# Two graph layers: counts in three slots in the first pass, one-hots in the fourth slot's room, selection matrices with edges side by side

## The chip, the cores and the metric

One core of a Trainium2 chip runs the whole kernel. The metric is device microseconds of one execution. Before the change it is 4469.84 us, the median of three runs (4464.91 to 4476.29).

## What is computed

Two graph layers over 12500 nodes of 64 features and 212500 edges, sorted by destination. Cut to what matters:

```python
h = maximum(layernorm(x), 0)
msg = h[src] + edge_attr                        # first layer, 64 features per edge
agg = segment_sum(msg, dst)
h = relu(agg @ W1 + b1) @ W2 + b2               # 64 -> 128 -> 64
x = x + batchnorm(h) * gamma + beta
h = maximum(layernorm(x), 0)
for W, b in ((W11, b11), (W12, b12)):           # second layer, two convolutions
    h = relu(segment_sum((h @ W)[src] * dis[src] * dis[dst], dst) + b)   # self loop added
x = x + graphnorm(h)
```

`dis` is one over the root of a node's degree. So three times the rows of a node table are summed over the edges that end in a node: passes 0, 1 and 2.

## The kernel before

**How a pass sums.** The nodes are cut into 100 tiles of 125. A table row is held as three bf16 parts (high, middle, low), 192 columns, and a column of ones counts edges. A pass has two ways to sum. A *dense window* (125 destination nodes) multiplies a matrix of edge counts, 125 x 12500 in fp8, with the whole table that lies in SBUF: 100 products (L1102, "app"). The other edges go in *groups* of 1280 (128 partitions x 10): GpSimd gathers their rows by ten indirect DMAs (L1265), VectorE makes a selection matrix of 96 columns per ten edges of a partition (L964, "S"), and ten products (L1124) add them. `DENSE = (54, 69, 69)` windows are dense in passes 0, 1 and 2. In pass 0 all 167 groups need a selection matrix, since the edge features of every edge are summed too: SP loads 320 KB of them (L1299, "edges"), VectorE makes the middle and low parts (L980, "rest1", "rest2") and ten products (L1117) sum them. 79 of the 167 groups of pass 0 are gathered as well, alternating with groups that are not, and the last ones are not.

**How the counts are built.** All windows of pass 0 and 17 windows of pass 1 are built on the chip, the others are loaded from the `counts` memory (1600 KB each, L1288). A window takes 32 products (L1084, "bld") of two one-hot matrices, both by VectorE: `oh` of 200 columns (L954, one per product, `NOH = 6` buffers) and `ob` (L951, one for four products, `NOB = 3` buffers). Two products fill one of two PSUM banks (`NBANK = 2`), and ScalarE copies the pair into the window's slot (L1204, "evict"). There are `NA = 4` slots of counts, `part(o_A, slot, n_A)`. A finished window is stored for the passes behind it (L1303, "keep").

**What follows the sums.** VectorE folds the three parts of a window (L996, L997) or group (L987), TensorE turns the fold (L1189, L1185), and VectorE adds it to `acc` (L1020, L1015). In pass 0 each finished run of 500 nodes goes through the perceptron: L1137 and L1140 on TensorE, then relu (L1213), hout (L1217), hmean (L1222) and hvar (L1227) on ScalarE.

**What sets the order.** `make_plan` writes every engine's list by hand: each piece of work has a due time in plan units (one window is `NAP = 25` units, the products of one window 1 unit per four), and an engine's list is sorted by it. In pass 0 a one-hot is due 3.3 units ahead of its product, S 7.0, the edge DMA 12.5, rest1 5.2 and rest2 4.2 ahead of the group's products. Within its list an engine waits on semaphores: a one-hot for the product that used its buffer (`p_bld`), a product for its one-hot (`v_oh`) and for the eviction two pairs back (`a_ev`), the edge DMA for the products of group v-2 (`p_q`), a slot for the products of the window that had it (`p_app`) and for its store (`st_cnt`). After pass 0, SP loads x again into `H`, which is the room of slots 2 and 3 (L1338); VectorE uses it from L1602 on, behind the batch norm.

## Time and profile before

| | |
|---|---|
| median of three runs | 4469.84 us |
| the profiled execution | 4486.21 us, its span 4484.9 us |
| pass 0 (first fold at 219, last at 1880) | about 1670 us from 210 us |
| batch norm, second layer norm, until the first fold of pass 1 | 148 us |
| pass 1, pass 2 | about 1232 us, 1140 us |
| PE busy | 3012.4 us, 67% of the span |
| DVE busy | 1926.5 us, 43% |
| POOL busy | 1861.6 us, 42% |
| ACT busy | 796.3 us, 18% |
| mean granted TensorE clock | 0.81 |

The profile is one execution. Its groups ("lines") give busy time, the mean duration of one instruction, and the idle time of the engine just before the group's instructions with what ended it. PE is TensorE's matmul, PEld its weight load, which runs beside the matmul before it. Busy times of PE groups overlap each other, since a matmul's record holds its latency. "remote" and "issue" are waits whose end the profile can't put down to a recorded instruction. The granted clock is 1.00 at 2.4 GHz and 0.50 at 1.2 GHz.

### The profile page before, as it was taken

The numbers are of one execution on the slowest core, as the hardware profiler recorded it, in microseconds if no ns is written. First come the engines' busy times: TensorE is split into PE (matmuls) and PEld (weight loads), VectorE is DVE, ScalarE is ACT, GpSimd is POOL, SyncE is SP. The second block draws the span as 40 slices with busy tenths as digits, with TensorE's granted clock in tenths as the row PEclk, the third lists the DMA queues.
The fourth block names the chain that finished last, engine by engine and source line by source line (L and its number), as shares of the span: only waits on it lengthen the run. The fifth ranks groups of instructions, "written<-read, shape, count | busy, mean of one in ns | idle before, by whom it ended". The sixth has DMA issues, their size and how long they took to land.

```text
span 4484.9 us, 66591 instructions
## 1 busy us (share of the span) xinstructions
PE 3012.4 (67%) x26545; PEld 2766.3 (62%) x26545; DVE 1926.5 (43%) x4856; ACT 796.3 (18%) x1708; POOL 1861.6 (42%) x1895
## 2 busy tenths in 40 slices
PE   1366676676666667737777777777847777776777
PEld 1365565566556556636666676666846666666667
DVE  9476676767667667742333332323301111111112
ACT  6122222222222223332111111111100000000000
POOL 4554444545444442032444433444134444444441
PEclk9988788878877788858778878888968778878878
DMA  5243333434334333443333333333443333333334
GB/s 125 78 115 100 96 111 99 118 96 116 99 94 114 96 111 101 118 124 119 113 99 114 127 99 127 100 116 126 140 120 113 126 111 127 113 111 119 119 126 123
DMA packets 359879, 504.29 MB, mean 112 GB/s; under 512 B 302486, under 2 KB 302679, under 8 KB 334736
## 3 DMA queue, kind: packets, MB, share of 16 engines
q1 hardware_dynamic: 298437, 402.60, 27.6%
q0 software_dynamic: 60512, 94.12, 9.3%
q8 instruction: 219, 3.59, 0.3%
q10 hardware_dynamic: 616, 3.20, 0.3%
q14 instruction: 95, 0.78, 0.1%
HBM read 362.65 MB, written 137.13 MB: 111 GB/s over the span
## 4 chain that ended last, share of the span: by engine, by line
PE 50%; another core or an unknown queue 17%; issue 14%; DVE 13%; ACT 3%; DVEq 1%; DMA 1%; SPq 0%; POOL 0%; ACTq 0%; POOLq 0%
PE psum L1102 34%; PE psum L1084 6%; DVE arena L954 4%; PE psum L1124 3%; PE psum L1117 3%; DVE arena L980 2%; DVE arena L951 2%; ACT arena L1204 1%; DVEq L1013 1%; PE psum L1067 1%; DVE arena L964 1%; PE psum L1189 1%; PE psum L1137 1%; PE psum L1185 1%
## 5 line engine op out<-in xcount | busy, mean ns | idle before, releaser
L1265 POOL DMA_INDIRECT arena<-table,srcT x1840 | 1800.2, 978 | 2300.3 <-PE psum L1124 1638.2
L1102 PE MATMUL psum<-arena 125*125 125x193 bf16 (+1 forms) x19200 | 2374.5, 274 | 404.9 <-issue 356.6
L1102 PEld LDWEIGHTS psum<-arena 125*125 125x125 fp8e4 x19200 | 2108.8, 157 | 499.6 <-issue 460.6
L1084 PE MATMUL psum<-arena 128*125 128x200 f16 x2272 | 609.0, 287 | 594.4 <-issue 263.0
L954 DVE TENSOR_SCALAR arena<-iota,keyT,oddT 128x200 f16<-128x200 f16 x2272 | 700.8, 336 | 613.2 <-remote 374.4
L1204 ACT CAST arena<-psum 125x400 uint16<-125x400 f32 x1136 | 549.4, 492 | 2148.3 <-PE psum L1084 1236.2
L1084 PEld LDWEIGHTS psum<-arena 128*125 128x125 f16 x2272 | 344.5, 157 | 686.5 <-DVE arena L954 359.4
L951 DVE TENSOR_TENSOR arena<-modT,psum 128x500 f16<-128x500 f16 x568 | 376.4, 663 | 0.1
L964 DVE SCALAR_TENSOR_TENSOR arena<-relT,psum 128x960 bf16<-128x960 f16 x272 | 310.8, 1143 | 0.0
L997 DVE TENSOR_REDUCE arena<-psum 125x64 f32<-125x192 f32 x192 | 67.2, 350 | 562.5 <-PE psum L1102 288.8
L980 DVE TENSOR_TENSOR arena<-arena 128x650 f32<-128x650 f32 (+1 forms) x334 | 274.4, 822 | 7.0 <-DMA arena<-in_edge_attr_dram 4.8
L1117 PE MATMUL psum<-arena 128*96 128x195 bf16 (+1 forms) x1662 | 215.0, 285 | 2.3 <-DVE arena L980 2.3
L1247 ACT ACTIVATE cneg<-cst 125x1 f32<-125x1 f32 x25 | 5.1, 203 | 1189.8 <-DVE arena L1039 1039.0
L987 DVE TENSOR_REDUCE arena<-psum 96x65 f32<-96x195 f32 (+1 forms) x275 | 96.5, 351 | 273.2 <-PE psum L1124 270.9
L1124 PE MATMUL psum<-arena 128*96 128x192 bf16 x1846 | 198.6, 258 | 3.9 <-DMA arena<-table,srcT 3.9
L1117 PEld LDWEIGHTS psum<-arena 128*96 128x96 bf16 (+1 forms) x1662 | 191.1, 145 | 2.8 <-issue 2.5
L1189 PE MATMUL psum<-ident,arena 125*64 125x125 f32 x192 | 60.5, 315 | 190.3 <-DVE arena L997 117.6
L1124 PEld LDWEIGHTS psum<-arena 128*96 128x96 bf16 x1846 | 177.3, 132 | 4.4 <-DMA arena<-table,srcT 4.2
L996 DVE COPY cnt<-psum 125x1 f32<-125x1 f32 x123 | 19.4, 158 | 371.9 <-remote 217.5
L1020 DVE SCALAR_TENSOR_TENSOR acc<-psum,acc 64x125 f32<-64x125 f32 x192 | 53.3, 277 | 270.0 <-remote 192.4
L1015 DVE SCALAR_TENSOR_TENSOR acc<-psum,acc 65x96 f32 (+1 forms) x275 | 68.6, 249 | 205.3 <-PE psum L1185 146.2
L1189 PEld LDWEIGHTS psum<-ident,arena 125*64 125x64 f32 x192 | 23.5, 122 | 215.2 <-issue 188.5
(207 smaller groups left out, 1000.2 us busy)
## 6 DMA issues: line engine op xcount, KB each, us to landing
arena<-counts SPq DMA_DIRECT2D x121, 1600.0 KB
counts<-arena SPq DMA_DIRECT2D x71, 1600.0 KB
arena<-in_edge_attr_dram SPq DMA_DIRECT2D x166, 320.0 KB
arena<-table,srcT POOLq DMA_INDIRECT x1840
table<-arena SPq DMA_DIRECT2D x8, 1050.0 KB
table<-arena SPq DMA_DIRECT2D x25, 168.0 KB
arena<-table SPq DMA_DIRECT2D x4, 1050.0 KB
arena<-in_x_dram ACTq DMA_DIRECT2D x4, 700.0 KB
```

The source lines that it names most:

```text
L951: dve.tensor_tensor(ob(four % NOB), mod, it, ALU.is_equal)
L954: dve.tensor_scalar(oh(v % NOH), iota1[:, :], keyT[:, v:v + 1], oddT[:, v:v + 1], ALU.is_equal, ALU.mult).then_inc(v_oh, 1)
L964: dve.scalar_tensor_tensor(out=S, in0=rel, scalar=0.0, in1=it, op0=ALU.add, op1=ALU.is_equal).then_inc(v_S, 1)
L980: dve.tensor_tensor(ebuf(e, i + 1)[0:parts, 0:nt * FE], a, upper, ALU.subtract).then_inc(v_rest1 if i == 0 else v_rest2, 1)
L987: dve.tensor_reduce(qbuf(n % 2)[:, 0:fe], ps_q.rearrange("p (s f) -> p f s", s=3)[:, 0:fe, :], X, ALU.add).then_inc(v_fq, 1)
L1084: pe.matmul(to, ob(v // NB4 % NOB)[:, v % NB4, :], oh(v % NOH).rearrange("p (j m) -> p j m", m=2), start=True, stop=True).then_inc(p_bld, 1)
L1102: last = pe.matmul(ps_v[n % 2][0:PN, 0:xc], A(slot)[0:PN, j, 0:PN], Xs[0:PN, j, 0:xc], start=(j == 0), stop=(j == J - 1))
L1117: last = pe.matmul(ps_q, S[0:parts, t, :], e3(v % NEDGE)[0:parts, t, :, :], start=(t == 0), stop=(t == nt - 1 and not gathered))
L1124: last = pe.matmul(to, S[0:parts, t, :], gbuf(slot)[0:parts, t, :].rearrange("p (s f) -> p s f", s=3), start=(k > 0 and t == 0), stop=(t = ...
L1189: pe.transpose(ps_g[0:F, 0:PN], vbuf(m % 2)[0:PN, :], ident[0:PN, 0:PN]).then_inc(p_win, 1)
L1204: act.copy(A2(slot)[0:PN, :, i // 2 * SUB:(i // 2 + 1) * SUB], ps_b[b // 2 % NBANK][0:PN, :].rearrange("p (j x) -> p j x", x=SUB)).then_in ...
L1265: pool.indirect_dma_start(out=gbuf(slot)[0:parts, t, :], out_offset=None, in_=tables[k], in_offset=bass.IndirectOffsetOnAxis(ap=idx, axis= ...
```

## The change

Pass 0 has 53 dense windows and uses three slots for counts (`NA0 = 3`). The room of the fourth holds 14 more `oh` buffers and 4 more `ob` buffers in pass 0 (`NOH = (20, 6)`, `NOB = (7, 3)`) and a constant `wide` (0 to 95, each ten times). One-hots of pass 0 are due 14 units ahead of their product in place of 3.3, S 10, rest1 8.2, rest2 7.2 and the edge DMA 14.5 units. With 53 windows 80 groups of pass 0 are gathered, and pass 1 builds 18 windows, one at every third place from the seventh. The selection matrix of pass 0 is stored with the ten edges side by side (96 x 10 in place of 10 x 96) and made by a two-input comparison of `relT`, turned the same way, with `wide`, both fp16 in SBUF; the products read it with a step of ten elements. hmean and hvar are due 7.3 and 7.4 units behind, in place of 6.2 and 6.4. The reload of x waits for the last build and the last selection matrix of pass 0.

```diff
 NS = 2
-NOH = 6
+NOH = (20, 6)
 NB4 = 4
-NOB = 3
+NOB = (7, 3)
 NA = 4
+NA0 = 3
 NBANK = 2
 TURN_GAP = 2.6
-DENSE = (54, 69, 69)
+DENSE = (53, 69, 69)
...
         for q in range(D):
-            if n_b < len(built) and q >= 6 and (q - 5) * len(built) >= n_b * (D - 7):
+            if n_b < len(built) and q >= 6 + 3 * n_b:
...
                     act.append((t + 0.2, "evict", (b, q, i)))
-                dve.append((t - 3.3, "oh", b))
+                dve.append((t - (14.0 if k == 0 else 3.3), "oh", b))
...
         pe.append((t, "grp", n))
-        dve.append((t - 7.0, "S", n))
+        dve.append((t - (10.0 if k == 0 else 7.0), "S", n))
         if k == 0:
-            sp.append((t - 12.5, "edges", n))
-            dve.append((t - 5.2, "rest1", n))
-            dve.append((t - 4.2, "rest2", n))
+            sp.append((t - 14.5, "edges", n))
+            dve.append((t - 8.2, "rest1", n))
+            dve.append((t - 7.2, "rest2", n))
...
             act.append((t + 6.0, "hout", i))
-            act.append((t + 6.2, "hmean", i))
-            act.append((t + 6.4, "hvar", i))
+            act.append((t + 7.3, "hmean", i))
+            act.append((t + 7.4, "hvar", i))
...
         def oh(k):
-            return part(o_oh, k, n_oh).bitcast(F16)
+            at = part(o_oh, k, n_oh) if k < NOH[1] else part(o_ox, k - NOH[1], n_oh)
+            return at.bitcast(F16)
...
-            return part(o_ob, k, n_ob).bitcast(F16).rearrange("p (n d) -> p n d", d=PN)
+            o = o_ox + (NOH[0] - NOH[1]) * n_oh
+            at = part(o_ob, k, n_ob) if k < NOB[1] else part(o, k - NOB[1], n_ob)
+            return at.bitcast(F16).rearrange("p (n d) -> p n d", d=PN)
...
+        def sbuf_w(n):
+            return part(o_S, n, NT * W // 2).bitcast(BF16).rearrange("p (w t) -> p w t", t=NT)
...
+        wide = arena[:, o_wide:o_wide + W * NT // 2].bitcast(F16).rearrange("p (w t) -> p w t", t=NT)
...
                     V(dve.memset(ebuf(q).rearrange("p (t f) -> p t f", f=FE)[:, :, F:FE], 1.0))
+                dve.wait_ge(a_hi, NCH)
+                V(dve.tensor_copy(wide, iota[:, 0:W].rearrange("p (w a) -> p w a", a=1).broadcast_to([P, W, NT])))
...
             return (P, NT) if g < G else (R, 2)
+        def slot_of(k, q):
+            return q % NA0 if k == 0 else (plans[k]["s0"] + q) % NA
...
                         dve.wait_ge(st_x1, NCH * NBAND * 16)
+                    noh, nob = NOH[k], NOB[k]
                     if v % NB4 == 0:
                         four = v // NB4
-                        if four >= NOB:
-                            dve.wait_ge(p_bld, NB4 * (four - NOB + 1))
+                        if k == 1 and v == pl["b"]:
+                            dve.wait_ge(p_bld, NB0)
+                        if four >= nob:
+                            dve.wait_ge(p_bld, NB4 * (four - nob + 1))
                         mod = modT[:, v:v + NB4].rearrange("p (n a) -> p n a", a=1).broadcast_to([P, NB4, PN])
                         it = ps_i[:, 0:PN].rearrange("p (a d) -> p a d", a=1).broadcast_to([P, NB4, PN])
-                        dve.tensor_tensor(ob(four % NOB), mod, it, ALU.is_equal)
-                    if v >= NOH:
-                        dve.wait_ge(p_bld, v - NOH + 1)
-                    dve.tensor_scalar(oh(v % NOH), iota1[:, :], keyT[:, v:v + 1], oddT[:, v:v + 1], ALU.is_equal,
+                        dve.tensor_tensor(ob(four % nob), mod, it, ALU.is_equal)
+                    if v >= noh:
+                        dve.wait_ge(p_bld, v - noh + 1)
+                    dve.tensor_scalar(oh(v % noh), iota1[:, :], keyT[:, v:v + 1], oddT[:, v:v + 1], ALU.is_equal,
...
-                    S = sbuf(n % NS)
-                    if g < G:
-                        rel = relT[:, :, g:g + 1].broadcast_to([P, NT, W])
-                        it = ps_i[:, 0:W].rearrange("p (a w) -> p a w", a=1).broadcast_to([P, NT, W])
-                        dve.scalar_tensor_tensor(out=S, in0=rel, scalar=0.0, in1=it, op0=ALU.add,
-                                                 op1=ALU.is_equal).then_inc(v_S, 1)
+                    if k == 0:
+                        parts, nt = shape(g)
+                        rel = relT[:, g, :] if g < G else relh_l[0:R, :]
+                        rel = rel.rearrange("p (a t) -> p a t", a=1).broadcast_to([parts, W, nt])
+                        dve.tensor_tensor(sbuf_w(n % NS)[0:parts, :, 0:nt], rel, wide[0:parts, :, 0:nt],
+                                          ALU.is_equal).then_inc(v_S, 1)
                     else:
-                        rel = relh_l[0:R, :].rearrange("p (t a) -> p t a", a=1).broadcast_to([R, 2, W])
-                        it = ps_i[0:R, 0:W].rearrange("p (a w) -> p a w", a=1).broadcast_to([R, 2, W])
-                        dve.scalar_tensor_tensor(out=S[0:R, 0:2, :], in0=rel, scalar=0.0, in1=it, op0=ALU.add,
-                                                 op1=ALU.is_equal).then_inc(v_S, 1)
+                        parts, nt = shape(g)
+                        rel = relT[:, g, :] if g < G else relh_l[0:R, :]
+                        rel = rel.rearrange("p (t a) -> p t a", a=1).broadcast_to([parts, nt, W])
+                        it = ps_i[0:parts, 0:W].rearrange("p (a w) -> p a w", a=1).broadcast_to([parts, nt, W])
+                        dve.scalar_tensor_tensor(out=sbuf(n % NS)[0:parts, 0:nt, :], in0=rel, scalar=0.0, in1=it,
+                                                 op0=ALU.add, op1=ALU.is_equal).then_inc(v_S, 1)
...
                     to = ps_b[pair % NBANK][0:PN, :].rearrange("p (j s m) -> p j s m", s=2, m=2)[:, :, s, :]
-                    pe.matmul(to, ob(v // NB4 % NOB)[:, v % NB4, :], oh(v % NOH).rearrange("p (j m) -> p j m", m=2), start=True,
+                    pe.matmul(to, ob(v // NB4 % NOB[k])[:, v % NB4, :],
+                              oh(v % NOH[k]).rearrange("p (j m) -> p j m", m=2), start=True,
...
-                    slot = (pl["s0"] + q) % NA
+                    slot = slot_of(k, q)
...
                     parts, nt = shape(g)
-                    S = sbuf(n % NS)
+                    S = sbuf_w(n % NS).rearrange("p w t -> p t w") if k == 0 else sbuf(n % NS)
...
                     n = pl["d0"] + q
-                    slot = (pl["s0"] + q) % NA
+                    slot = slot_of(k, q)
                     if i == 1:
-                        if q >= NA:
-                            act.wait_ge(p_app, n - NA + 1)
+                        if q >= (NA0 if k == 0 else NA):
+                            act.wait_ge(p_app, n - (NA0 if k == 0 else NA) + 1)
...
                 sp.wait_ge(p_app, D0 - 2)
-                for i in (2, 3):
-                    sp.wait_ge(st_cnt[i], kept[0][i])
+                sp.wait_ge(p_bld, NB0)
+                sp.wait_ge(v_S, NG)
+                sp.wait_ge(st_cnt[2], kept[0][2])
...
```

## Rows read from the trace of the kernel before

**Rows 1.** Totals by stretch: us, PE, PEld, DVE, ACT, POOL busy (count), clock, DMA, GB/s

```profile
300.00:1700.00 1400.00, 932.57 (x7822) 839.35 (x7821) 975.57 (x2483) 370.53 (x799) 667.56 (x650) 0.81 0.38 105
1770.00:1880.00 110.00, 90.11 (x865) 81.27 (x863) 96.73 (x252) 37.89 (x83) 0.00 (x0) 0.94 0.47 140
2100.00:3150.00 1050.00, 768.47 (x6832) 714.91 (x6830) 328.32 (x960) 137.89 (x295) 433.06 (x457) 0.80 0.35 113
3400.00:4350.00 950.00, 685.29 (x6131) 637.20 (x6130) 115.06 (x278) 14.47 (x54) 424.11 (x450) 0.80 0.36 117
```

**Rows 2.** The same view, while the first gathers are issued

```profile
115.00:142.00 27.00, 6.87 (x35) 5.15 (x33) 8.24 (x20) 1.98 (x5) 20.30 (x22) 1.00 0.23 51
142.00:174.00 32.00, 0.56 (x2) 0.28 (x2) 2.30 (x4) 0.48 (x1) 19.80 (x21) 1.00 0.21 44
```

**Rows 3.** Timeline, 140 to 176 us: start, us, engine, line, [idle before <-releaser]

```profile
142.62 0.56 PE L1084 MATMUL psum<-arena 128*125 128x200 f16 x2 [5.10 <-issue]
...
166.96 0.94 POOL L1265 DMA_INDIRECT arena<-table,srcT  x1 [0.30 <-issue]
...
172.30 0.33 DVE L954 TENSOR_SCALAR arena<-iota,keyT,oddT 128x200 f16<-128x200 f16 x1 [28.33 <-remote]
174.40 0.49 ACT L1204 CAST arena<-psum 125x400 uint16<-125x400 f32 x1 [31.92 <-remote]
...
175.03 0.56 PE L1084 MATMUL psum<-arena 128*125 128x200 f16 x2 [31.85 <-ACT arena L1204]
```

**Rows 4.** Groups by form, 300 to 1700 us: busy, mean ns | idle before <-releasers

```profile
L1102 PE MATMUL psum<-arena 125*125 125x193 bf16 x4275 | 605.0, 278 | 1.4 <-issue 1.4
...
L954 DVE TENSOR_SCALAR arena<-iota,keyT,oddT 128x200 f16<-128x200 f16 x1365 | 426.8, 339 | 403.6 <-remote 231.7 <-PE psum L1084 154.5 <-issue 15.3
L1084 PE MATMUL psum<-arena 128*125 128x200 f16 x1368 | 363.3, 288 | 401.7 <-issue 179.7 <-ACT arena L1204 172.4 <-DVE arena L954 48.6
L1204 ACT CAST arena<-psum 125x400 uint16<-125x400 f32 x685 | 331.1, 492 | 1031.1 <-PE psum L1084 609.3 <-remote 393.5 <-issue 25.2
L951 DVE TENSOR_TENSOR arena<-modT,psum 128x500 f16<-128x500 f16 x341 | 226.2, 663 | 0.0
L980 DVE TENSOR_TENSOR arena<-arena 128x650 f32<-128x650 f32 x260 | 214.5, 825 | 4.5 <-DMA arena<-in_edge_attr_dram 2.4 <-issue 1.9
...
L964 DVE SCALAR_TENSOR_TENSOR arena<-relT,psum 128x960 bf16<-128x960 f16 x129 | 147.6, 1144 | 0.0
L1117 PEld LDWEIGHTS psum<-arena 128*96 128x96 bf16 x1290 | 147.4, 144 | 0.1
L1124 PE MATMUL psum<-arena 128*96 128x192 bf16 x640 | 73.9, 270 | 0.0
...
L997 DVE TENSOR_REDUCE arena<-psum 125x64 f32<-125x192 f32 x43 | 14.8, 344 | 0.0
L1189 PE MATMUL psum<-ident,arena 125*64 125x125 f32 x43 | 13.8, 322 | 16.9 <-DVE acc L1015 14.2 <-issue 2.7
L1227 ACT ACTIVATE arena<-acc,hneg 64x500 f32<-64x500 f32 x19 | 13.5, 712 | 0.6
...
L1137 PEld LDWEIGHTS psum<-acc,w 64*128 64x128 f32 x38 | 7.4, 243 | 22.5 <-DVE acc L1015 18.1 <-issue 4.2
```

**Rows 5.** The same view, 1770 to 1880 us, no gathers

```profile
L1084 PE MATMUL psum<-arena 128*125 128x200 f16 x130 | 31.3, 263 | 7.3 <-DVE arena L954 5.1 <-ACT arena L1204 2.3
...
L1137 PE MATMUL psum<-acc,w 64*128 64x500 f32 x4 | 3.1, 874 | 4.0 <-DVE acc L1015 4.0
```

**Rows 6.** The same view, 2100 to 3150 us, pass 1

```profile
L1102 PE MATMUL psum<-arena 125*125 125x193 bf16 x5571 | 693.6, 276 | 110.3 <-issue 107.3
```

**Rows 7.** The same view, 3400 to 4350 us, pass 2

```profile
L1102 PE MATMUL psum<-arena 125*125 125x192 bf16 x5438 | 632.8, 276 | 175.0 <-issue 172.7
```

**Rows 8.** Timeline, 1858 to 1896 us: the reload of x and its first user

```profile
1866.83 2.22 SPq L1338 DMA_DIRECT2D arena<-in_x_dram  x2
...
1895.80 0.62 DVE L1602 TENSOR_TENSOR arena<-psum,arena 125x448 f32<-125x448 f32 x1 [3.43 <-PE psum L1585]
```

39 lines of the change are left out of this document (22 added, 17 removed).

## The prediction

> **What bounds the kernel now.** I read the totals by stretch first, because the passes have different limits. In the first pass (300 to 1700 us) TensorE is busy 932.57 of 1400 us and VectorE 975.57, so neither is full [rows 1]. The reader is to see which work is going on when TensorE is idle: in 1770 to 1880 no gather is issued and TensorE is busy 90.11 of 110 us. The other two passes, where VectorE has little to do, still leave TensorE idle (1050 - 768.47 = 282 us, 950 - 685.29 = 265 us) while gathers are issued [rows 1].
>
> The start of the pass shows it alone. Gathers are issued back to back until 168 us [rows 3]. TensorE is busy 6.87 of the 27 us from 115, then 0.56 of 32 us [rows 2]. In the timeline the two builds of 142.62 us are answered by VectorE's next one-hot only at 172.30 and by ScalarE's next eviction at 174.40, both released by TensorE, and TensorE goes on at 175.03 [rows 3]. So TensorE's completions come late while gathers run, and no queue in front of it had run dry. Idle TensorE per gathered group of ten: (1400 - 932.57) / 65 = 7.2 us in the first pass, 265 / 45 = 5.9 us in the third, which builds nothing and makes its few selection matrices with time to spare [rows 1].
>
> What ends TensorE's idle time in the first pass is read in the groups: nearly all stands before L1084, the build (401.7 us of 467), named issue 179.7, ScalarE's eviction 172.4, VectorE's one-hot L954 48.6. L954 itself waited 403.6 us, 386 of them for TensorE or for an unseen releaser, and the eviction L1204 1031 us [rows 4]. A build needs the eviction of two pairs before (NBANK = 2) besides its one-hot. That loop is four products long, shorter than the six one-hots, and the change leaves it as it is.
>
> **The change part by part** (minus is time saved; against the profiled execution, 4486.2 us, which lies 16.4 us above the median).
>
> *53 dense windows instead of 54.* Removed: 100 L1102 and 32 L1084, one fold, one turn. The groups' busy times overlap, so I scale: the eight costliest PE groups of the stretch, L1102 (605.0) to L1189 (13.8), add up to 1313 us for 932.57 busy, a factor 0.71 [rows 1, 4]. Of the 1313, L1102 and L1084 are 968.3 [rows 4]; 968.3 x 0.71 / 43 windows (L997 x43) = 16.0, with the turn 16.2: **-16.2 us**. Added: one more gathered group. Its selection matrix and edge sums exist already; new are ten L1124 (73.9 x 0.71 / 64 = 0.8 us) and one gather run at 7.2: **+8.0**. Keeping three slots: an eviction into a slot waits for the products of three windows back, which end 19 of 25 plan units before it, and for its store, some 48 units before; a window takes 1400 / 43 = 32.6 us, so 19 units are 25 us, against a longest late answer of 32 us at the start, where no slot is reused. Nothing.
>
> *Twenty one-hots and seven sets of four, made 14 units ahead.* This takes away waits of L1084 on L954 and the swing of VectorE. Upper bound where gathers run: 48.6 x 1670 / 1400 = 58 us; lower: nothing, since the eviction stands behind the same late signal. I take **-10**, near the lower end, because L954 was waiting for TensorE and not busy (403.6 us) [rows 4]. VectorE's folds and additions stay in its queue behind one-hots that wait for a build 20 back instead of 6 back; the place in plan time that this wait needs (0.8 units before the fold's own matmuls end, now 1.0) is the same.
>
> *Selection matrices, first pass.* 167 times 1144 ns for 960 elements [rows 4]. Bounds: 1144 (no faster form) and, if two elements go per cycle, the price of L951, 663 ns for 500 elements [rows 4]. I take 660, so VectorE is freed of 167 x 0.48 = 80 us. It counts only where VectorE is the slower one: 1770 to 1880 us, where it is busy 96.73 of 110 [rows 1] and TensorE's idle time of 19.9 us has L954 and folds behind it (L1084 5.1, L1137 4.0 [rows 5]). Gather-free windows are about five; with the deeper lead **-8** (bounds 0 and -20 for this stretch and its like).
>
> The Trainium skill ("VectorE: DVE Perf Modes", the perf-mode tier table) has a 16 bit two-input operation from SBUF at two elements per cycle and any with a PSUM operand at one. By that the new matrix would take 657 ns as an estimate from its fixed 151 cycles; no row of before shows the fast form.
>
> *The weights' layout.* The same matrices are TensorE's stationary operand: 96 columns now lie 10 elements (20 bytes) apart. Some 1662 + 792 = 2454 loads. Today's contiguous load is 144 ns for 96 columns and the dearest one in the trace is the fp32 load, 243 ns for 128 columns, 182 for 96 [rows 4]. So a load costs between 0 and 38 ns more, 0 to 93 us in all. I take **0**: loads are issued beside the product before, and L1117's weight load shows no idle time of its own (0.1 us). Below nothing is excluded, for a scattered read is not cheaper than a packed one.
>
> *ScalarE's statistics a unit later.* Mean and square after each perceptron chunk (712 ns the square [rows 4]) stop standing right behind hout, before an eviction. 25 chunks x at most 0.9 us = 22; most evictions are waiting anyway: **-3**. The perceptron's next relu waits for the square two chunks back, far off.
>
> *Second pass.* One window more is built (18 for 17) and stands 3 windows from the next. Pass two takes 1050 / 55.7 = 18.9 us per window, pass three 950 / 54.4 = 17.5 [rows 1, 6, 7]; 1.4 x 69 / 17 = 5.6 us per built window is an upper bound, for the node work is in it too. **+5**. One load of 1600 KB less.
>
> *Costed at nothing.* The constant of 960 elements before the first one-hot: 1.1 us by L964, hidden since TensorE then waits for the first gather run until 175 [rows 3]; uncovered 1.1. The reload of x now waits for the last selection matrix and the last build as well: it was issued at 1866.83, and its first user at 1895.80 was released by TensorE, not by it [rows 8]; the SP queue still has the last edges and the last store in front of it, so it moves by 3 us at most. Edges and remainders 3 units earlier: the DMA for group v can only start when group v-2 is through, 16 units before; VectorE waited 2.4 us for edges in 130 groups [rows 4], so the cover is ample, and if it is gone, folds and additions queue behind the remainder's wait.
>
> Sum: -16.2 + 8.0 - 10 - 8 - 3 + 5 = **-24.2 us**: 4462 for the profiled execution, 4469.8 - 24.2 = 4446 at the median. What is late next: TensorE in gather runs, as before.
>
> **The rivals.**
> 1. *The depth pays in the gather runs.* If the 1.3 us per group by which the first pass is worse than the third (7.2 against 5.9) is VectorE's coupling, 79 groups give 103 us, 93 beyond the 10 counted: 4446 - 93 = 4353. For it: L954 is named for 48.6 us of L1084's waits. Against: the eviction loop is shorter and untouched, and rows 3 show both answers arriving together.
> 2. *Scattered weights cost more than they hide (slower).* Place: L1117 and L1124 loads of the first pass; price up to 38 ns x 2454 = 93 us, 4446 + 93 = 4539; it decides from where a load outlasts the product beside it. For it: no load of the kernel is scattered today, so nothing shows it to be free. Against: TensorE overlaps loads of 125 columns with products without a gap. The Trainium skill ("SBUF — State Buffer", Door 1: The DMA port swizzle, note on cachelines) says that reads want two hits in each 16 byte line, or 8 bf16 at most between them. By that rule a step of 20 bytes pays on every column and the time is this rival's; no row here shows a step over 4 bytes.
> 3. *Nothing of the queueing shows.* VectorE's lead was never what ended a wait and the gather-free stretch is too short: -16.2 + 8 + 5 = -3, 4467.
>
> **How the numbers follow.** Forecast 0.50 at 4446 (its own range 4430 to 4465), rival 1 0.17 at 4353, rival 2 0.15 at 4539, rival 3 0.18 at 4467. A measurement of this kernel can tell about 0.3% (13.4 us) from no change. Faster: 0.35 of the forecast and rival 1, 0.52. Within: 0.15 of the forecast and 0.12 of rival 3, 0.27. Slower: rival 2 and 0.06 of rival 3, where an edge wait eats the gain, 0.21. The range, 4370 to 4505, takes in forecast, rival 3 and partial forms of the other two, and leaves out the full ones. Predicted: 4446 us, -0.5%.
>
> **What would show it.** L964's successor near 660 ns, not 1144. TensorE's idle time per gathered group still near 7 us, before L1084, ended by evictions; near 6 says rival 1. L954 still waits for TensorE, only further ahead. TensorE's pitch inside groups of ten wider than now says rival 2. Window pace without gathers down by 1 to 2 us. The prediction is wrong if TensorE's silence in gather runs depends on how much VectorE has queued, or if scattered weights are slow.

## The result and the profile after

The changed kernel takes **4512.9 us** (median of four runs, 4509.9 to 4528.2) where the kernel before takes 4467.4 beside it (4462.9 to 4476.3): a ratio of 1.0101, 95% interval 1.0074 to 1.0128. It is 45 us slower, where 24 us faster had been forecast, and 8 us above the upper end of the forecast's range. The profiled execution is 4528.2 us, its span 4526.5.

The totals by stretch of the changed kernel are these (us busy and instruction counts by engine, then granted clock, DMA share, GB/s); they answer [rows 1].

```profile
300.00:1700.00 1400.00, 1006.91 (x7514) 924.88 (x7514) 888.52 (x2383) 354.72 (x766) 654.73 (x629) 0.81 0.35 100
1770.00:1880.00 110.00, 96.05 (x821) 88.85 (x821) 94.64 (x267) 42.03 (x93) 16.40 (x16) 0.95 0.39 121
2100.00:3150.00 1050.00, 769.77 (x6788) 719.35 (x6789) 358.93 (x1061) 158.63 (x341) 420.32 (x443) 0.79 0.34 113
3400.00:4350.00 950.00, 683.65 (x6108) 633.99 (x6107) 116.02 (x280) 15.27 (x57) 423.27 (x450) 0.80 0.36 117
```

In the first pass TensorE is busy 74 us longer in the same 1400 us and gets fewer instructions done (7514; the row of before has its count too), and 629 gathers are issued for 650. VectorE is 87 us less busy. Per group of ten gathers: busy 1006.91 / 62.9 = 16.0 us for 932.57 / 65 = 14.3, idle (1400 - 1006.91) / 62.9 = 6.25 us for 7.2. Passes are measured here from the first to the last fold of a dense window (the table of times ahead counts passes 1 and 2 otherwise). The first pass lasts 1690.9 us for 1660.8, with a window fewer; the second 1243.7 for 1220.9; the third, whose program is the same, 1172.9 for 1173.7. So the loss stands in the first pass (30 us) and the second (23 us), less 9 us in the work between the two (139.4 for 148.2).

The groups by form in 300 to 1700 us, which answer [rows 4] (L1110 is the build, L1144 and L1151 the products of edge features and of gathered rows, L988 the selection matrix):

```profile
L1292 POOL DMA_INDIRECT arena<-table,srcT x629 | 654.9, 1041 | 745.5 <-PE psum L1151 572.4 <-issue 173.1
L978 DVE TENSOR_SCALAR arena<-iota,keyT,oddT 128x200 f16<-128x200 f16 x1304 | 412.9, 339 | 459.4 <-PE psum L1110 235.5 <-remote 212.8 <-issue 8.4
L1110 PE MATMUL psum<-arena 128*125 128x200 f16 x1305 | 347.0, 289 | 346.5 <-issue 148.8 <-ACT arena L1231 118.7 <-DVE arena L978 78.9
L1144 PE MATMUL psum<-arena 128*96 128x195 bf16 x1260 | 233.4, 340 | 0.0
L1144 PEld LDWEIGHTS psum<-arena 128*96 128x96 bf16 x1260 | 221.8, 261 | 0.4
L1151 PE MATMUL psum<-arena 128*96 128x192 bf16 x630 | 114.7, 334 | 0.0
L988 DVE TENSOR_TENSOR arena<-relT,arena 128x960 bf16<-128x960 f16 x126 | 81.6, 647 | 0.0
```

Of the kernel before, in the same stretch:

```profile
L1117 PE MATMUL psum<-arena 128*96 128x195 bf16 x1290 | 165.3, 283 | 0.0
```

The selection matrix takes 647 ns for 1144. A scattered load (columns 20 bytes apart) takes 261 ns where the packed one took 144, and the product behind it 340 ns for 283: 233.4 / 1260 - 165.3 / 1290 = 57 ns more of TensorE's busy time for each product of edge features, and 114.7 / 630 - 73.9 / 640 = 67 ns for each of gathered rows. VectorE waits for TensorE as before.

### The profile page after: what moved, and what is told of

Read it like the earlier page. It is cut to its first block, busy times and chain, and to the rows that moved or that the text cites. A ratio compares the mean times of both kernels' runs of the same rounds, so it can differ in the third digit from the quotient of the medians.

```text
span 4526.5 us, 66413 instructions
## 1 busy us (share of the span) xinstructions
PE 3137.3 (69%) x26454; PEld 2903.0 (64%) x26454; DVE 1855.5 (41%) x4854; ACT 794.5 (18%) x1708; POOL 1888.1 (42%) x1905
## 4 chain that ended last, share of the span: by engine, by line
PE 57%; another core or an unknown queue 18%; issue 12%; DVE 7%; ACT 3%; DMA 1%; DVEq 1%; SPq 0%; POOL 0%; ACTq 0%; POOLq 0%
PE psum L1129 36%; PE psum L1110 7%; PE psum L1144 5%; PE psum L1151 5%; DVE arena L978 2%; ACT arena L1231 1%; PE psum L1093 1%; DVE arena L975 1%; DVEq L1039 1%; PE psum L1216 1%; PE psum L1167 1%; PE psum L1212 1%; PE psum L1164 1%; DVE arena L1006 0%
## 5 line engine op out<-in xcount | busy, mean ns | idle before, releaser
L1292 POOL DMA_INDIRECT arena<-table,srcT x1850 | 1827.2, 988 | 2343.1 <-PE psum L1151 1681.9
L1110 PE MATMUL psum<-arena 128*125 128x200 f16 x2272 | 606.4, 286 | 547.6 <-issue 257.6
L978 DVE TENSOR_SCALAR arena<-iota,keyT,oddT 128x200 f16<-128x200 f16 x2272 | 705.5, 336 | 659.8 <-remote 340.0
L1110 PEld LDWEIGHTS psum<-arena 128*125 128x125 f16 x2272 | 345.2, 158 | 638.9 <-issue 352.7
L1144 PE MATMUL psum<-arena 128*96 128x195 bf16 x1662 | 308.1, 339 | 4.0 <-DVE arena L1006 4.0
L1144 PEld LDWEIGHTS psum<-arena 128*96 128x96 bf16 x1662 | 292.5, 261 | 4.8 <-issue 4.2
L1006 DVE TENSOR_TENSOR arena<-arena 128x650 f32<-128x650 f32 x334 | 274.5, 822 | 7.2 <-DMA arena<-in_edge_attr_dram 6.9
L1151 PE MATMUL psum<-arena 128*96 128x192 bf16 x1856 | 251.4, 285 | 0.3 <-issue 0.3
L1151 PEld LDWEIGHTS psum<-arena 128*96 128x96 bf16 x1856 | 233.6, 183 | 0.7 <-DMA arena<-table,srcT 0.5
L995 DVE SCALAR_TENSOR_TENSOR arena<-relT,psum 128x960 bf16<-128x960 f16 x106 | 120.8, 1140 | 0.0
```

Source lines behind the costliest of these rows:

```text
L978: dve.tensor_scalar(oh(v % noh), iota1[:, :], keyT[:, v:v + 1], oddT[:, v:v + 1], ALU.is_equal, ALU.mult).then_inc(v_oh, 1)
L995: dve.scalar_tensor_tensor(out=sbuf(n % NS)[0:parts, 0:nt, :], in0=rel, scalar=0.0, in1=it, op0=ALU.add, op1=ALU.is_equal).then_inc(v_S, 1)
L1006: dve.tensor_tensor(ebuf(e, i + 1)[0:parts, 0:nt * FE], a, upper, ALU.subtract).then_inc(v_rest1 if i == 0 else v_rest2, 1)
L1110: pe.matmul(to, ob(v // NB4 % NOB[k])[:, v % NB4, :], oh(v % NOH[k]).rearrange("p (j m) -> p j m", m=2), start=True, stop=True).then_inc(p ...
L1144: last = pe.matmul(ps_q, S[0:parts, t, :], e3(v % NEDGE)[0:parts, t, :, :], start=(t == 0), stop=(t == nt - 1 and not gathered))
L1151: last = pe.matmul(to, S[0:parts, t, :], gbuf(slot)[0:parts, t, :].rearrange("p (s f) -> p s f", s=3), start=(k > 0 and t == 0), stop=(t = ...
```

## The experiments

They ran on five chips, always beside the kernel before. **The runs are of two kinds**, and no number below is to be read without this: on two chips the kernel before takes 4355 and 4358 us, near the 4467 of the result; on three others 2997 to 3000 us. In the first kind TensorE falls silent: it idles in runs of gathers as in [rows 3]. In the second it hardly does. All runs of the first kind, the result's too, were made before all runs of the second, and none of the five chips ran in both times, so that chip and time can't be told apart; "kind" stands for either. All ratios are to the kernel before on the same chip, and times are compared on one chip unless the text says otherwise.

| kernel before | runs on that chip |
|---|---|
| 4355 us | packed_slow, before_scattered, packed_row, old_spacing |
| 4358 us | packed_psum_tt, before_spaced, packed_shallow, after_again |
| 2998 us | before_spaced2, after_spaced2, row_spaced2, scattered_slow |
| 2999.6 us | after_third, scattered_slow2, packed_slow2, packed_deep_oh |
| 2996.6 us | pairs2, after_shallow |

### One part at a time, where TensorE falls silent (kernel before 4355 and 4358 us)

**packed_slow** has the old matrix and the old layout, with all else of the change (`...` marks what is left out, here and below).

```diff
-                    S = sbuf_w(n % NS).rearrange("p w t -> p t w") if k == 0 else sbuf(n % NS)
+                    S = sbuf(n % NS)
...
-                    if k == 0:
-                        ... tensor_tensor(sbuf_w(n % NS), rel, wide, ALU.is_equal)
+                    dve.scalar_tensor_tensor(out=sbuf(n % NS)[0:parts, 0:nt, :], in0=rel, scalar=0.0, in1=it,
```

> The changed kernel with one thing undone: in the first pass the selection matrix is stored packed again (tile, then column) and so made by the old operation with its PSUM operand (1144 ns by the trace of before, against 647 after); 53 windows, 20 one-hots, three slots and the spacing of the second pass stay. Theory A (the scattered stationary operand is what was lost): the loads of L1144 and L1151 are back at 141 to 144 ns from 261, their products at about 283 and 270 ns from 340 and 334, and the time falls below the kernel before: 4467 - 24 + 8 (the slow matrix where VectorE is the slower one) + 18 (second pass) = about 4470 at worst and 4420 at best. Theory B (the loss comes from the second pass and the deeper queue, the scattered loads being hidden beside products): loads are faster but the time stays within 10 us of 4513.

Measured: 4409.7, ratio 1.0137 (1.0072 to 1.0201). Theory A's numbers for the loads hold (138 and 135 ns), its time doesn't: the loss is still there without scattered loads.

**before_scattered**: the kernel before, its old operation writing through `sbuf_w(n % NS).rearrange("p w t -> p t w")`.

> The kernel before with one thing done: in the first pass the old operation writes its selection matrix scattered (columns 20 bytes apart), and TensorE loads it so; nothing else. The operation itself should stay near 1144 ns, since a PSUM operand already holds it at one element per cycle. Theory A: some 1290 + 640 products in 300 to 1700 us take 57 and 67 ns more of TensorE each, 95 + 53 = 148 us in the pass, of which what stands in the idle time of gather runs (467 of 1400 us) may vanish: +60 to +148 us, 4527 to 4615. Theory B: 4467 within 13 us.

Measured: 4554.6, 1.0469 (1.0419 to 1.0519). The expectation of 1144 ns was wrong, and so this was no look at the layout alone: with each element written 20 bytes from the last, the operation takes nearly four times as long.

```profile
L968 DVE SCALAR_TENSOR_TENSOR arena<-relT,psum 128x960 bf16<-128x960 f16 x125 | 553.4, 4427 | 0.0
```

**packed_row**: packed, two SBUF inputs, `tensor_tensor(sbuf(n % NS), rel, row, is_equal)` with each remainder repeated 96 times (step 0) and `row` = 0 to 95.

> The changed kernel with the matrix packed (tile, then column) but made from 16 bit inputs in SBUF: the remainder is repeated along the inner dimension with step 0 and the constant is one row of 96. This tells whether the fast form of VectorE needs the scattered layout at all. If a repeated element is served at two per cycle, L986's successor takes about 650 ns and the time is that of packed_slow or some 10 us less; if it is not, the operation takes 1000 to 1150 ns and the time is that of packed_slow.

Measured: 4196.5, **0.9646** (0.9574 to 0.9718), 213 us below packed_slow, though its operation is no faster; both expectations were for packed_slow's time. The gain is in the first pass (1421.2 us for 1630.1); the second and third take 1252.1 and 1145.1 us for 1244.0 and 1149.6. The two kernels' rows, packed_slow first, both 300 to 1700 us (packed_row's first pass ends at 1627 us):

```profile
L1285 POOL DMA_INDIRECT arena<-table,srcT x666 | 683.6, 1026 | 716.5 <-PE psum L1144 532.3 <-issue 182.6 <-remote 1.7
L988 DVE SCALAR_TENSOR_TENSOR arena<-relT,psum 128x960 bf16<-128x960 f16 x133 | 152.1, 1144 | 0.0
L1103 PE MATMUL psum<-arena 128*125 128x200 f16 x1375 | 367.0, 289 | 411.8 <-ACT arena L1224 206.2 <-issue 155.6 <-DVE arena L978 49.2
```

```profile
L1292 POOL DMA_INDIRECT arena<-table,srcT x672 | 808.2, 1203 | 406.7 <-PE psum L1151 210.4 <-issue 193.5 <-remote 2.8
L989 DVE TENSOR_TENSOR arena<-relT,arena 128x960 bf16<-128x960 f16 x147 | 168.7, 1147 | 0.0
L1110 PE MATMUL psum<-arena 128*125 128x200 f16 x1508 | 377.0, 273 | 200.2 <-issue 93.6 <-ACT arena L1231 78.8 <-DVE arena L978 26.7
```

The gathers are what differs: 1203 ns each for 1026, and TensorE's wait before a build is halved (200.2 us before 1508 builds, 411.8 before 1375). In packed_row's timeline one sees a gather held up while L989 runs:

```profile
700.78 0.95 POOL L1292 DMA_INDIRECT arena<-table,srcT  x1 [0.30 <-issue]
702.03 2.25 POOL L1292 DMA_INDIRECT arena<-table,srcT  x1 [0.30 <-issue]
702.32 1.14 DVE L989 TENSOR_TENSOR arena<-relT,arena 128x960 bf16<-128x960 f16 x1
```

In the whole first pass the 168 gathers that overlapped L989 took 1.62 us in the mean, the 132 that overlapped packed_slow's L988 0.95. All gathers of the pass together were busy 882 us for 745, 137 us more, and the pass was 209 us shorter.

**packed_psum_tt**: packed_row with its second input in PSUM.

> packed_row won 213 us over packed_slow though its matrix takes as long (1147 ns against 1144). The two differ in the operation (tensor_tensor for scalar_tensor_tensor) and in the second input (a row in SBUF for one in PSUM). Here the operation is tensor_tensor and the row stays in PSUM. If two SBUF inputs matter (they hold up the gathers that GpSimd issues meanwhile: 1.62 us each beside L989 of packed_row, 0.95 beside L988 of packed_slow), this is packed_slow: 1.014 of the kernel before. If the operation's kind matters, it is packed_row: 0.965.

Measured: 4408.2, 1.0121 (1.0068 to 1.0175). As a ratio it is packed_slow's (1.0137, on the other chip of this kind): the second SBUF input matters, the operation's kind doesn't.

**before_spaced**: four writes of 16 unused counts behind each gather.

```diff
+                    for _ in range(4):
+                        pool.wait_ge(k_fill, filled[0])
+                        pool.iota(filler[:, :], pattern=[[1, 16]], base=0, channel_multiplier=0).then_inc(k_fill, 1)
```

> The kernel before with its gathers spread: behind every gather of the three passes GpSimd writes four small rows of counts that nobody reads, so that one gather follows the next after some 2 us instead of 1.25; nothing else changes and nothing is left out. Theory S (TensorE falls silent because ten gathers come at 1.25 us each, and packed_row won because its matrix spreads them): TensorE's silence in the runs of gathers (7.2 us per gathered group in the first pass, 5.9 in the third) falls by half or more, so 185 groups x 3 us or more = at least 500 us less: below 0.90. At the least as much as packed_row, 0.965. Theory T (the silence goes with the number of gathers, not with their pace, and packed_row won otherwise): 1.00, or above where later gathers make the groups wait (up to 185 x 7 us = 1.29).

Measured: 4017.3, **0.9227** (0.9179 to 0.9275), 341 us less, though GpSimd does more. Theory S holds in kind and in its lesser number, not in its larger one, for a new wait took the place of the silence. Little is left of the wait before the build (41.9 us for 401.7 in [rows 4]), and TensorE waits for gathered rows instead:

```profile
L1085 PE MATMUL psum<-arena 128*125 128x200 f16 x1439 | 363.9, 278 | 41.9 <-DVE arena L955 31.2 <-ACT arena L1205 5.9 <-issue 2.9
L1125 PE MATMUL psum<-arena 128*96 128x192 bf16 x690 | 121.3, 357 | 288.2 <-DMA arena<-table,srcT 288.2
```

In its timeline a gather follows the last after 1.9 us:

```profile
699.46 0.95 POOL L1266 DMA_INDIRECT arena<-table,srcT  x1 [1.38 <-issue]
700.42 0.79 POOL L1273 IOTA filler<- 128x16 int32 x4
701.35 0.98 POOL L1266 DMA_INDIRECT arena<-table,srcT  x1
```

The second and third pass gain nearly all: 1219.3 us to 1037.9 (against before_scattered, whose second pass is that of before, on the other chip) and 1144.9 to 1033.9 (against after_again, whose third pass is the same program, on this chip), some 290 of the 341 us. Their bound is now another one: in 3100 to 3900 us 42 groups take 800 / 42 = 19.0 us each, which is ten gathers of 1.9 us, and all of TensorE's wait there, 218.1 us, is for gathered rows. So in this kind TensorE's silence depends on the pace of the gathers and is there at 1.25 us; packed_row fits this, since what holds GpSimd up spreads them.

**packed_shallow**: packed_slow with `NOH = (6, 6)`, `NOB = (3, 3)` and the old due times.

> packed_slow (packed matrix by the old operation) with the depth undone too: 6 one-hots and 3 sets of four in every pass, and the old due times of one-hots, matrices, edges and remainders. 53 windows in three slots, the later statistics and the second pass stay as changed. Theory C (building ahead costs time by itself, since VectorE's work moves into other stretches, and packed_slow's first pass was some 50 us longer than that of the kernel before): 1.000 to 1.006 of the kernel before, about 25 to 50 us below packed_slow. Theory D (depth is worth something, as forecast, and the loss is in the fifty-fourth window made dense in the second pass and one more gathered group): 1.014 or above.

Measured: 4350.4, 0.9977 (0.9945 to 1.0010). That is theory C, and a little better. The clean partner is packed_psum_tt, on the same chip and equal to packed_slow in ratio: building ahead (the deeper buffers and the earlier due times together) costs 4408.2 - 4350.4 = **58 us** here, and in the two profiled executions the first pass is 1636.1 us long for 1565.4.

```profile
L1110 PE MATMUL psum<-arena 128*125 128x200 f16 x1273 | 342.2, 291 | 384.2 <-ACT arena L1231 168.6 <-issue 158.1 <-DVE arena L978 56.7
```

```profile
L1103 PE MATMUL psum<-arena 128*125 128x200 f16 x1329 | 348.8, 284 | 330.9 <-issue 157.7 <-ACT arena L1224 118.7 <-DVE arena L978 52.6
```

```profile
300.00:1600.00 1300.00, 869.40 (x7335) 784.70 (x7336) 917.61 (x2324) 344.41 (x746) 624.60 (x611) 0.80 0.38 106
```

```profile
300.00:1600.00 1300.00, 901.35 (x7648) 812.21 (x7646) 953.41 (x2426) 359.57 (x777) 665.55 (x642) 0.82 0.40 110
```

(The build in 300 to 1600 us of packed_psum_tt, then of packed_shallow; then the totals of the two, in the columns of [rows 1].) The cost is idle time of TensorE: per gathered group (1300 - 869.40) / 61.1 = 7.05 us with the deep queue and (1300 - 901.35) / 64.2 = 6.21 without, times 80 groups 67 of the 71 us; busy time is 14.2 and 14.0.

Of what ends the wait before a build, nearly only ScalarE's share is less with the shallow queue. The eviction answers TensorE's late completions, so this shows where the time is and not why.

The traces bear on one reason. The remainders ("rest1", "rest2") read two SBUF inputs as L989 does: in packed_slow's first pass the 196 gathers beside one took 1.24 us, the others 0.95. With the shallow queue 240 gathers are beside a remainder and with the deep one 206, and the gathers of the pass are busy 755 us for 742. At packed_row's rate (209 us won for 137 us more of gathers) these 13 us are worth some 20 of the 71 us. That is an estimate; the rest is unexplained.

**after_again** and **old_spacing**: the changed kernel; and the same with `(q - 5) * len(built) >= n_b * (D - 7)` put back.

> The changed kernel itself, on the chip of the three runs beside it, so that they can be compared with it. Theory: 1.010 of the kernel before, as measured. packed_slow and before_scattered were run on a faster chip (4355 us for the kernel before), and by them the loss is made of two parts: everything but the layout and the operation +55 us (packed_slow), and the scattered layout with the fast operation about -12 (4355 x 1.0101 = 4399 against 4410).

> The changed kernel with the spacing of the built windows of the second pass put back to the even spread (one in 3.65 windows, to the end of the pass, instead of one in 3 and none in the last eleven). Theory: the second pass, first fold to last, went from 1221 to 1244 us; of that about 5 us belong to the eighteenth built window, 18 to the spacing. So 4513 - 18 = 4495. Rival: the spacing costs nothing and the 23 us are the window itself and its one-hots: 4513 within 5 us.

Measured: 4414.1, 1.0146 (1.0091 to 1.0200); and 4422.3, 1.0175 (1.0126 to 1.0225). The spacing is no cause: the second pass is 1237.4 us with the old one, 1244.0 in packed_slow and 1219.3 in before_scattered, which builds 17 windows, all three on one chip. The eighteenth built window itself costs 18 to 25 us, not 5.

### The same parts where TensorE doesn't fall silent (kernel before 3000 us)

**before_spaced2**, **after_spaced2**, **row_spaced2**: two filling writes behind each gather of the kernel before, of the changed one, of packed_row.

> The kernel before with two idle rows behind each gather instead of four: one gather in about 1.55 us (before 1.25, before_spaced 1.92). In before_spaced TensorE's silence was gone but it waited for gathered rows (288 us before L1125 in 300 to 1700 us, 218 in 3100 to 3900). If the silence goes with the pace steeply, most of that wait is won and none of the silence returns: 0.88 to 0.91 of the kernel before. If it returns in proportion (half way from 1.92 to 1.25), about 0.95 to 0.97.

> The changed kernel with the same two idle rows behind each gather. With the silence out of the way TensorE is nearer to its limit, so the scattered loads (261 ns against 144, some 60 ns more TensorE time for each of 2454 products, 148 us) show in full: 60 to 120 us above before_spaced2. If instead the fast matrix and the depth are what was held back by the silence, it is below before_spaced2.

> packed_row (packed matrix from two SBUF inputs, 1147 ns; all else as changed) with the same two idle rows behind each gather. If packed_row won only because its matrix spreads the gathers (theory S), its lead of 213 us over packed_slow is not added to what the idle rows win: within 40 us of before_spaced2, give or take the second pass. If it won in another way, it stays some 150 us below. Against after_spaced2 it differs in the layout and the operation alone: 60 to 140 us below.

Measured, beside 2998.0: 3241.5, 1.0821 (1.0801 to 1.0842); 3258.3, 1.0872; 3315.1, 1.1065. All three expectations missed, for they were made for the silent kind. With no silence to take away, a slower pace of gathers is pure loss: they come 1.47 us apart (median) for 1.25, 1.18 times as far, and before_spaced2's third pass takes 809.0 us for packed_slow2's 687.2, 1.18 times as long. So gathers bound it.

The scattered loads, which were to cost 60 to 120 us, show as 17 with all the rest of the change, and the second pass is 812.1 for 811.3: the eighteenth built window costs 1 us here. The order is turned round too: with two writes packed_row is 57 us behind the changed kernel, not 60 to 140 below it, for its matrix holds up gathers (1170 ns each for 1088, 300 to 1400 us) on the engine that is now the limit. packed_row without the writes never ran in this kind.

**after_third**, **scattered_slow2**, **packed_slow2**, **packed_deep_oh** stood side by side. after_third is the changed kernel, packed_slow2 is packed_slow again, and scattered_slow2 is scattered_slow: the scattered layout, but made by the old operation with `ps_i` as the second input, written in order of memory. packed_deep_oh is packed_slow with matrices, edges and remainders at their old due times.

> The changed kernel, as the mark for the three runs beside it. On a chip where TensorE falls silent in gather runs (kernel before 4350 to 4470 us): 1.010 to 1.015. On one where it doesn't (kernel before 2998 us), where scattered_slow was 0.9944: the fast operation frees VectorE of 80 us and is no longer paid for by anything, so 0.985 to 0.995; or no better than scattered_slow, since VectorE waits for TensorE there, 0.994.

> scattered_slow once more, beside packed_slow2. Only the layout differs between the two. Theory A (the dearer loads are paid, 261 ns against 144): 60 to 148 us above packed_slow2. Rival (the silence or the wait for gathers swallows them): within 15 us of packed_slow2.

> packed_slow once more (packed matrix, old operation, all else as changed), as the other end of the comparison. With silence: 1.014 as before. Without silence: if the scattered loads are paid in full, 60 us or more below scattered_slow2, so 0.975 or less where scattered_slow2 is 0.994.

> packed_slow with the places of selection matrices, edges and remainders in the first pass put back (7, 12.5, 5.2 and 4.2 units ahead); the 20 one-hots and seven sets of four, 14 units ahead, stay. Theory E (the two remainders of 825 ns, which read two SBUF inputs and hold up gathers as packed_row's matrix does, were moved out of the gather runs): it is as fast as packed_shallow, 0.998. Theory F (the depth of the one-hots itself costs): it stays at packed_slow, 1.012 to 1.014.

Measured, beside 2999.6:

| kernel | us | ratio | 95% interval |
|---|---|---|---|
| after_third (the change) | 2921.2 | **0.9737** | 0.9716 to 0.9758 |
| packed_slow2 | 2954.2 | 0.9847 | 0.9824 to 0.9870 |
| packed_deep_oh | 2968.9 | 0.9895 | 0.9874 to 0.9917 |
| scattered_slow2 | 2978.8 | 0.9933 | 0.9910 to 0.9957 |

The change is a gain of 78 us here. The scattered layout costs 2978.8 - 2954.2 = 25 us (the intervals leave some 10 either way), less than theory A's 60 and more than its rival's 15; the fast operation gives back 2978.8 - 2921.2 = 58; earlier matrices, edges and remainders are worth 15. Theories E and F were made for the silent kind and no run there decides between them. What the same program does in the two kinds is seen in the third pass, first of the result's kernel (3400 to 4350 us), then of after_third (2300 to 2800 us):

```profile
L1129 PE MATMUL psum<-arena 125*125 125x192 bf16 x5417 | 630.8, 276 | 173.5 <-issue 171.1
L1292 POOL DMA_INDIRECT arena<-table,srcT x450 | 424.5, 943 | 548.3 <-PE psum L1151 424.9 <-issue 123.4
```

```profile
2300.00:2800.00 500.00, 473.55 (x5467) 469.70 (x5466) 103.31 (x251) 13.66 (x51) 378.18 (x400) 0.98 0.61 199
L1129 PE MATMUL psum<-arena 125*125 125x192 bf16 x4843 | 428.6, 247 | 0.0
L1292 POOL DMA_INDIRECT arena<-table,srcT x400 | 378.4, 946 | 122.0 <-issue 122.0
```

Within a run, gathers take the same 0.94 us and come 1.25 us apart in both. In the second kind GpSimd never waits for TensorE: 400 gathers fill 500 us, TensorE idles 26.5 us of them and its granted clock is 0.98 for 0.80. A group takes 12.5 us for 950 / 45 = 21.1: of the 8.6 us between them 5.3 are idle time of TensorE and 3.4 its busy time; a product of counts takes 276 ns at the one clock and 247 at the other. The layout's cost is in the totals of 300 to 1100 us of packed_slow2 and scattered_slow2:

```profile
300.00:1100.00 800.00, 650.52 (x6208) 597.43 (x6207) 756.28 (x1971) 295.05 (x636) 589.09 (x541) 0.91 0.53 145
```

```profile
300.00:1100.00 800.00, 718.06 (x6139) 673.36 (x6138) 748.24 (x1947) 291.90 (x628) 561.43 (x533) 0.96 0.52 145
```

67.5 us more of TensorE in 800 us, at a better clock, filled idle time that stood at 149.5 us in packed_slow2 (the first row) and is 81.9, so only 1.1% fewer instructions were done.

**scattered_slow** had given the same on the chip of before_spaced2, where packed_slow did not run beside it:

> The changed kernel with its layout kept (columns 20 bytes apart for TensorE, written in order of memory) but made by the old operation with the row in PSUM, so near 1144 ns. before_scattered was no clean look at the layout, for its operation wrote with steps and took 4427 ns. Against packed_slow (1.014 of the kernel before) only the layout differs: theory A says 60 to 148 us more, 1.028 to 1.048; if the idle time in gather runs swallows the dearer loads, 1.014. Against the changed kernel (1.0146) it gives what the fast operation is worth.

Measured: 2979.2, 0.9944 (0.9927 to 0.9961).

**pairs2**: packed, with each remainder doubled first, so that all operands end in two neighbours.

```diff
+ dve.tensor_copy(rel2[0:pm, m % 2, 0:tm, :], one...broadcast_to([pm, tm, 2]))
+ rel = rel2[...].rearrange("p t (h a) -> p t h a", h=1).broadcast_to([parts, nt, W // 2, 2])
+ it = row[0:parts, :].rearrange("p (b h a) -> p b h a", b=1, a=2).broadcast_to([parts, nt, W // 2, 2])
```

(The copy runs one group ahead; its waits are left out.)

> The changed kernel with the matrix packed again, yet all three operands of its operation end in two neighbouring 16 bit elements: the ten remainders of a group are first doubled into a small row (one copy of 20 elements, some 100 ns a group), the constant is one row of 96, and output and weights are packed. If neighbouring pairs are enough for two elements per cycle, the operation takes about 650 ns and the loads are back at 141 ns: where TensorE isn't silent 0.974 x 3000 - 25 + 10 = 2906 (0.969); where it is silent, between packed_slow (1.014) and packed_row (0.965), since its matrix holds up gathers for 0.65 us, as the changed kernel's does. If pairs aren't enough (packed_row's repeated element wasn't), it takes 1150 ns: 0.985 to 0.99 where TensorE isn't silent, near packed_row (0.965 to 0.975) where it is.

Measured: 2933.7, 0.9781 (0.9764 to 0.9798), 300 to 1100 us:

```profile
L1007 DVE TENSOR_TENSOR arena<-rel,arena 128x960 bf16<-128x960 f16 x106 | 68.7, 648 | 0.0
L994 DVE COPY rel<-relT 128x20 f16<-128x20 f16 x106 | 20.0, 188 | 0.0
L1162 PEld LDWEIGHTS psum<-arena 128*96 128x96 bf16 x1060 | 105.9, 129 | 0.4 <-issue 0.2
L1169 PE MATMUL psum<-arena 128*96 128x192 bf16 x540 | 64.0, 274 | 49.1 <-DMA arena<-table,srcT 49.0
```

Both wishes came true, the fast operation and the packed load, and it is still 0.004 behind the change, which ran on another chip (0.9781 against 0.9737, each within 0.002): the freed TensorE waits for gathered rows, 49 us before L1169. The expected 0.969 left out that the gathers were next. From 300 to 1340 us they come 1.50 us apart in the mean, and 1.47 in after_third; 800 of them are 1202 and 1173 us, and the first passes are 1197.2 and 1177.9. Where the 0.03 us between gathers come from isn't shown; the gathers beside both the copy and L1007 took 1.38 us, those beside L1007 alone 1.17.

**after_shallow**: the change with the depth undone, as in packed_shallow.

> The changed kernel with the depth undone (6 one-hots, 3 sets of four, the old due times), its layout, operation and 53 windows kept. Where TensorE isn't silent (changed kernel 0.974): if building ahead is what lets VectorE carry the pass, 0.985 to 1.00; if it is worth nothing, 0.974. Where it is silent (changed kernel 1.0146, packed_slow 1.014 against packed_shallow 0.998): the depth costs the same 60 us here, 0.997 to 1.002; or nothing, 1.014.

Measured: 2992.2, 0.9989 (0.9978 to 1.0000). Against after_third's ratio on another chip, building ahead is worth 0.025, 75 us, where TensorE isn't silent; the first pass is 1177.9 us with it and 1242.9 without.

## Why the prediction was wrong

Two terms of the sum failed. Building ahead was put at -10 us with nothing as the worst case, and cost 58; the second pass was put at +5 and cost 18 to 25, which a better first pass made up for. Put together, in ratios to the kernel before:

| part | silent kind | other kind |
|---|---|---|
| 53 windows, three slots, statistics, second pass | -0.002 | not measured alone |
| building ahead | **+0.014** | **-0.025** |
| layout and operation | +0.003 | -0.011 (+0.008 and -0.019) |
| the change | +0.015, +0.010 in the result | -0.026 |

The silent column is from one chip (packed_shallow, packed_psum_tt, after_again); its differences are uncertain by some 0.005, and no run there undid the depth from the changed kernel itself. The other column's depth (after_shallow) is from another chip than the rest. Its parts leave +0.010 for the first row if they simply add, which isn't shown.

*53 dense windows, statistics, second pass.* Forecast -16.2 + 8.0 - 3 + 5 = -6 us; packed_shallow is -8 (its interval is -24 to +4). The sum came out right, in part by luck: inside it the second pass was mis-sized, 18 to 25 us (23 in the result) for +5 with an upper bound of 5.6. The bound divided the difference of two passes by the windows built. The window's price goes with the silence (1 us in after_spaced2); how is not shown.

*Depth.* This is the step that failed first. It said "lower: nothing, since the eviction stands behind the same late signal", and took -10. The runs of the silent kind show +58, outside the bounds: the deep queue makes TensorE's silence longer, by 0.84 us per gathered group. A reason why the gain could be nothing had been taken for a reason why a loss was impossible. Rival 1 (the depth pays in gather runs, 4353) is refuted in this kind; in the other, of which nothing could be known from the trace, the depth pays 75 us.

*The weights' layout.* "I take 0", bounds 0 to 38 ns for a load. The load costs 117 ns more, three times the upper bound, which had been taken from loads that differ in type and not in step. What it costs in time is another matter: 25 us, of 148 us more of TensorE's work (57 ns x 1662 + 67 x 792), measured only where TensorE isn't silent. Rival 2's sign for the load came true, its 4539 us did not come from it: with the packed layout back (packed_slow) the loss stays. By the rule of the Trainium skill ("SBUF — State Buffer", Door 1: The DMA port swizzle, note on cachelines) reads want two hits in each 16 byte line, so a step of 20 bytes pays on every column; the 261 ns for 144 agree.

*Selection matrices.* 660 ns was taken, 647 measured (1144 before). The Trainium skill ("VectorE: DVE Perf Modes", two elements per cycle by the perf-mode tier table, the 151 fixed cycles by its section on the TRN2 errata) gave 657 as an estimate. packed_row at 1147 ns shows that one element repeated with step 0 isn't served so, and pairs2 at 648 that rows of two neighbours are. Worth in time: forecast -8 with bounds 0 and -20; -58 in the other kind. In the silent kind layout and operation together are +0.003 (6 us), no more than the runs can tell from nothing. Unseen in the prediction was that an operation with two SBUF inputs holds up the gathers beside it. The Trainium skill says so ("SBUF — State Buffer", SBUF: two separate sides): two SBUF inputs of VectorE and a GpSimd operation that reads SBUF lock each other out. The 1.62 us against 0.95 agree. The trace of before had it already: in its first pass the 195 gathers beside L980, which reads two SBUF inputs, took 1.24 us, the others 0.95. The changed kernel's matrix does it too, so the +0.003 may be two effects that cancel: after_again's gathers are busy 761 us for packed_psum_tt's 742, worth some 29 us at packed_row's rate (an estimate), against a dearer layout.

*What bounds the kernel.* It was read rightly that TensorE's completions come late in gather runs, but their lateness was taken as fixed. It depends on the pace of the gathers, on the kind, and, as the forecast's last sentence on signs feared, in the silent kind on how much is built ahead (7.05 us per group in packed_psum_tt, 6.21 in packed_shallow).

*The signs to look for.* The matrix near 660 ns came true, and L978 still waits for TensorE (459 us): right. TensorE's idle time per gathered group was to stay near 7, and near 6 was to mean rival 1; it fell to 6.25 without rival 1's gain. Busy time rose by 1.7 us per group, so the likelier reading is that the wider pitch ate part of the silence, as rival 2 had it. The sign of the window pace without gathers can't be read in 1770 to 1880 us, where the changed kernel still issues 16 gathers.

**What stays open**: why the deep queue lengthens the first pass where TensorE is silent, the ScalarE share and the remainders' places being the only traces of it; what the silence is (in the third pass the 3072 byte packets of gathers take 0.217 us in the mean in the silent kind and 0.202 in the other); the layout's own cost in the silent kind; and whether the kinds are chips, times, or something else that ran beside them.

No version was found that beats both kernels everywhere. Where TensorE is silent before_spaced does (0.923), and packed_row (0.965); elsewhere the change itself is the best that ran. Two writes behind each gather never ran where TensorE is silent.

## What to carry to other kernels

Give an unseen cost a bound from a row that differs in the same respect (step, not type), and don't let "the gain may be nothing" become "there is no loss". When an engine idles without a queue in front of it, vary the pace of what runs beside it before anything is tuned around the gap: four idle writes between gathers were worth six times what the whole change moved on the same chip (341 us against 56). And run a change on more than one chip and at more than one time: the same one was 1% slower and 2.6% faster.

## What the runs showed of the hardware

- The same kernel (before) takes 4355 to 4467 us in some runs and 2997 to 3000 in others, on other chips and at a later time. In the changed kernel's third pass gathers (943 and 946 ns) and the selection matrix there (1139 and 1140 ns) are equally long in both; the difference is TensorE's silence while gathers are issued 1.25 us apart (idle (950 - 683.65) / 45 = 5.9 us per ten gathers against 26.45 / 40 = 0.7) and its lower granted clock (0.80 against 0.98), at which a product of counts takes 276 ns for 247.
- With the gathers about 1.9 us apart by work on GpSimd, nearly none of that silence is left (before_spaced: 41.9 us before the build for 401.7), and TensorE waits for the gathered rows instead (288.2 us).
- A weight load of 96 bf16 columns takes 260 to 262 ns with the columns 20 bytes apart, on five chips and in the result; packed it takes 129 to 146 ns in the first pass, and more only where its product waits for gathered rows (157 in row_spaced2, 188 in before_spaced).
- VectorE writing bf16 20 bytes apart takes 4427 ns for 960 elements, 1144 in order. A comparison of 960 elements with both inputs in SBUF takes 1147 ns when one input repeats an element with step 0 innermost, and 648 when it repeats rows of two neighbours.
- A gather is held up by a VectorE operation with two SBUF inputs (1.62 us beside one of 1147 ns, 1.24 beside one of 825 ns), not by one whose second input is in PSUM (0.95).
